# The largest-output pass of a quantized feed-forward layer: turned context split straight from PSUM by ScalarE and VectorE

## The chip, the cores and the metric

The program runs on one core of one Trainium2 chip. The metric is the device time of one execution in microseconds, the median over the runs shown.

## The reference, cut to what matters

The whole reference is two transformer layers. The pass that is changed is in the quantized feed-forward network of the first layer, and it also carries, beside it, the making of the second layer's keys.

```
# first layer's feed-forward network (act_qdq rounds to 16 bits with one scale for the whole tensor)
up   = act_qdq(x @ w_up.T)
gate = act_qdq(x @ w_gate.T)
gate = act_qdq(gate * fixed_qdq_u16(sigmoid(gate)))
o    = act_qdq(gate * up)          # its scale needs max |gate * up| over everything first
...
# second layer: q and k go through the same two projections
qp = (q @ W1.T + b1) @ W2.T + b2
kp = (k @ W1.T + b1) @ W2.T + b2   # k is ctx_1024, 16 x 256 rows of 512
```

The kernel folds both projections of q and k into one 512x512 matrix (`gram`) that is applied to the turned (transposed) context. The products are made in fp32r with operands split in a high part (the value rounded to fp32r) and a low part (value minus high part).

## The kernel before

`output_maximum` is the pass that finds the largest output. Its main loop runs over N = 48 pieces n of 128x1024 elements. Three engines work on a piece. SyncE (SP, the DMA queue) loads `raw(n)` (512 KB, two buffers) and, for odd n, the rounded sigmoids `sq(n)` (256 KB, one buffer). ScalarE (ACT) makes `up(n)` and, once VectorE has made the product, `gate(n)`; for odd n it also makes a sigmoid. VectorE (DVE) does, in its iteration n: for even n `rounded(n + 2)`; then `outputs(n)`, then `products(n + 2)`, then `largest(n)`. So `products(n)` is done in VectorE's iteration n - 2.

Beside it the second layer's keys are made. The context is 16 blocks x of 256 rows; a chunk c is two blocks. For each block SP loads `cin` (512 KB, one buffer), TensorE turns it into `ctp` in PSUM (`turn(x)`, 8 transposes), and it is split in a high and a low part in `cT` (memory of `qf_wd`, two buffers by c). In a chunk TensorE does turn(2c+2), key tile 0, key tile 1, turn(2c+3), key tiles 2 and 3, and the key biases `tb`; each tile is 12 matmuls of 128x512. ScalarE takes each key tile out of PSUM (`keys`) and SP stores it (256 KB).

What sets the order is the program order of each queue and the semaphores:

- In the version before, ScalarE copies `ctp` to `craw` in SBUF (L1587) and frees the PSUM by that (`c_out`); GpSimd (POOL) makes the high part by a cast (L1694) and the low part by a subtraction (L1696). `turn(x)` waits for `c_out`, x times.
- ScalarE does the copy for block x >= 2 in its piece n = 11 + 2x (`context_due`).
- SP works through its pieces in order. In piece n = 10 + 2x it issues raw(n), then `load_context(x)`, then a store of keys; in piece n = 11 + 2x it issues raw(n), then sq(n). `load_context(x)` waits until turn(x-1) is done, since there is one `cin`, and everything behind it in SP's queue waits with it:

```
if context_due(n + 1):
    load_context(context_due(n + 1))
...
def load_context(x):
    if x:
        sp.wait_ge(c_full, x)
```

Of the kernel before, what the change touches and what calls it, by code (L numbers as in the profile page):

```python
# [14 lines left out]
ALU = mybir.AluOpType  # L15
ACT = mybir.ActivationFunctionType
F32 = mybir.dt.float32
# [6 lines left out]
P = 128  # L24
B, S, D = 16, 256, 512
TOK = B * S
CT = 512
NCH = TOK // CT
NT = CT // P
KD = D // P  # L30
# [1396 lines left out]
def output_maximum(nc, a, ctx_in, keys_d, bias_d, raw_up, gate, sq_d, big, scal, folds, wd, wd_parts, wd_late, ident):  # L1427
# [9 lines left out]
    with Phase(nc, "om") as ph:  # L1437
# [13 lines left out]

        gram = ph.sb("gram", [P, 2, KD, D], F32R)
        cin = ph.sb("cin", [P, NK, D])
        craw = ph.sb("craw", [P, KD, S])
        rout = ph.sb("rout", [P, 2, CT])
        b12 = ph.sb("b12", [P, 2, KD])
        bsum = ph.sb("bsum", [P, KD])
# [16 lines left out]
            ph.sem(n) for n in ("turned", "turned_out", "m_full", "m_out", "beta_full", "beta_out", "g_full", "g_out", "gc_full", "gc_out"))  # L1474
        cleared, beta_ready, betas_ready, gram_hi, gram_low, gbraw_done, gb_hi, gb_low = (
            ph.sem(n) for n in ("cleared", "beta_ready", "betas_ready", "gram_hi", "gram_low", "gbraw_done", "gb_hi", "gb_low"))
        c_full, c_out, c_hi, c_low, r_full, r_out, t_full, t_out = (
            ph.sem(n) for n in ("c_full", "c_out", "c_hi", "c_low", "r_full", "r_out", "t_full", "t_out"))
        t_stored = [ph.sem(f"t_stored{i}") for i in range(2)]
        r_stored = [ph.sem(f"r_stored{i}") for i in range(2)]  # L1480

# [15 lines left out]
        with nc.Block() as block:  # L1497
# [69 lines left out]
            @block.scalar  # L1567
            def _(act):
                def sigmoid(n):
                    if n >= 2:  # L1570
                        act.wait_ge(sq_done, n // 2)
                    act.activation(sig[:], place(n), ACT.Sigmoid, scale=scal[:, S_G:S_G + 1]).then_inc(sig_ready, 1)

                def products(n):
                    s = n % 2
                    act.wait_ge(raw_ready[s], 16 * (n // 2) + 16)
                    if n >= 2:
                        act.wait_ge(out_done, n - 1)
                    act.activation(up[:, s, :], raw[:, s, :], ACT.Copy, scale=scal[:, I_U:I_U + 1]).then_inc(up_ready, 1)
                    act.wait_ge(prod_done, n + 1)  # L1580
                    act.activation(place(n), prod[:, s, :], ACT.Copy, scale=scal[:, I_A:I_A + 1]).then_inc(gate_ready, 1)

                def context(x):
                    act.wait_ge(c_full, x + 1)
                    if x:
                        act.wait_ge(c_low, x)
                    act.activation(craw[:], ctp[:], ACT.Copy).then_inc(c_out, 1)  # L1587

                def keys(c, i):
                    act.wait_ge(r_full, KD * c + i + 1)  # L1590
                    if c == 0 and i == 0:
                        act.wait_ge(gc_out, 2)
                        act.wait_ge(gb_low, 1)
                    if KD * c + i >= 2:
                        act.wait_ge(r_stored[i % 2], 16 * (2 * c + i // 2))
                    act.activation(rout[:, i % 2, :], rb[i][:], ACT.Identity, bias=gcol[:, i:i + 1]).then_inc(r_out, 1)

                def key_biases(c):
                    act.wait_ge(t_full, c + 1)
                    if c >= 2:  # L1600
                        act.wait_ge(t_stored[c % 2], 16 * (c // 2))
                    act.activation(trow[:, c % 2, :], tb[0:1, :], ACT.Identity, bias=bb[0:1, 0:1]).then_inc(t_out, 1)

                sigmoid(0)
                sigmoid(2)
                for n in range(N):
                    products(n)
                    if n % 2 and n + 3 < N:
                        sigmoid(n + 3)
                    if n == TURNED:  # L1610
                        for k in range(KD):
                            act.wait_ge(turned, k + 1)
                            act.activation(w2T[:, k, :], rb[k][:], ACT.Copy).then_inc(turned_out, 1)
                    if n == 3:
                        context(0)
                    if FOLDED <= n < FOLDED + KD:
                        act.wait_ge(m_full, n - FOLDED + 1)
                        act.activation(m[:, n - FOLDED, :], rb[n - FOLDED][:], ACT.Copy).then_inc(m_out, 1)
                    if n == 9:
                        act.wait_ge(beta_full, 1)  # L1620
                        act.activation(bsum[:], tb[:, 0:KD], ACT.Copy).then_inc(beta_out, 1)
                        context(1)
                    if 10 <= n < 10 + KD:
                        act.wait_ge(g_full, n - 9)
                        act.activation(graw[:, n - 10, :], rb[n - 10][:], ACT.Copy, scale=SCALE).then_inc(g_out, 1)
                    if n == 14:
                        act.wait_ge(gc_full, 1)
                        act.activation(gcol[:], tb[:, 8:8 + KD], ACT.Copy, scale=SCALE).then_inc(gc_out, 1)
                        act.activation(bb[:], tb[:, 16:17], ACT.Copy, scale=SCALE).then_inc(gc_out, 1)
                    if bias_due(n) is not None:  # L1630
                        key_biases(bias_due(n))
                    if keys_due(n):
                        keys(*keys_due(n))
                    if context_due(n):
                        context(context_due(n))
                key_biases(NCH - 1)

            @block.vector
            def _(dve):
# [6 lines left out]
                def products(n):  # L1646
                    s = n % 2
                    if s:
                        dve.wait_ge(sq_ready, 16 * (n // 2) + 16)
                    else:  # L1650
                        dve.wait_ge(sq_done, n // 2 + 1)
                    if n >= 2:
                        dve.wait_ge(gate_ready, n - 1)
                    dve.tensor_tensor(prod[:, s, :], place(n), sq[:, s, :], ALU.mult).then_inc(prod_done, 1)

                def outputs(n):
                    dve.wait_ge(gate_ready, n + 1)
                    dve.wait_ge(up_ready, n + 1)
                    if n:
                        dve.wait_ge(max_done, n)  # L1660
                    dve.tensor_tensor(outp[:], place(n), up[:, n % 2, :], ALU.mult).then_inc(out_done, 1)

                def largest(n):
                    dve.wait_ge(out_done, n + 1)
                    dve.tensor_reduce(mx[:, n:n + 1], outp[:], AX_X, ALU.max, apply_absolute_value=True).then_inc(max_done, 1)
# [4 lines left out]
                for n in range(N):  # L1670
                    if n % 2 == 0 and n + 2 < N:
                        rounded(n + 2)
                    outputs(n)
                    if n + 2 < N:
                        products(n + 2)
                    largest(n)
                dve.wait_ge(max_done, N)
                dve.tensor_reduce(mx_row[:], mx[:], AX_X, ALU.max).then_inc(row_max, 1)
# [5 lines left out]

            @block.gpsimd
            def _(pool):
                def context(x):
                    c, lo = x // 2, x % 2 * S
                    pool.wait_ge(c_out, x + 1)
                    if c >= 2:  # L1690
                        pool.wait_ge(t_full, c - 1)
                    if c == 1:
                        pool.wait_ge(gc_full, 1)
                    pool.tensor_copy(cT[c % 2][:, 0, :, lo:lo + S], craw[:]).then_inc(c_hi, 1)  # L1694
                    pool.wait_ge(c_hi, x + 1)
                    pool.tensor_tensor(cT[c % 2][:, 1, :, lo:lo + S], craw[:], cT[c % 2][:, 0, :, lo:lo + S].bitcast(F32), ALU.subtract).then_inc(c_low, 1)  # L1696

                pool.memset(betas, 1.0).then_inc(cleared, 1)
                pool.wait_ge(cleared, 1)
                pool.memset(gbraw, 1.0).then_inc(cleared, 1)  # L1700
                pool.wait_ge(cleared, 2)
                context(0)
                pool.wait_ge(b_ready, 32)
                pool.wait_ge(beta_out, 1)
                pool.tensor_tensor(beta[:], bsum[:], b12[:, 1, :], ALU.add).then_inc(beta_ready, 1)
                pool.wait_ge(beta_ready, 1)
                pool.tensor_tensor(betas, betas, beta[:].unsqueeze(2).broadcast_to([P, KD, P]), ALU.mult).then_inc(betas_ready, 1)
                context(1)
                for d in range(KD):
                    pool.wait_ge(g_out, d + 1)  # L1710
                    pool.tensor_copy(gram[:, 0, d, :], graw[:, d, :]).then_inc(gram_hi, 1)
# [6 lines left out]
                pool.tensor_copy(gb[:, 0], gbraw).then_inc(gb_hi, 1)  # L1718
                pool.wait_ge(gb_hi, 1)
                pool.tensor_tensor(gb[:, 1], gbraw, gb[:, 0].bitcast(F32), ALU.subtract).then_inc(gb_low, 1)  # L1720
                for x in range(2, 2 * NCH):
                    context(x)
                pool.wait_ge(row_max, 1)
                pool.partition_all_reduce(big[:, 0:1], mx_row[:], P, RMAX).then_inc(all_max, 1)

# [1 line left out]
            def _(pe):  # L1727
                def turn(x):
                    pe.wait_ge(c_ready, 16 * x + 16)
                    if x:  # L1730
                        pe.wait_ge(c_out, x)
                    for k in range(KD):
                        for t in range(NK):
                            ins = pe.transpose(ctp[:, k, t * P:(t + 1) * P], cin[:, t, k * P:(k + 1) * P], ident[:])
                    ins.then_inc(c_full, 1)
# [980 lines left out]
```

## Time and profile before

| what | value |
|---|---|
| median of 3 runs | 3637.34 us (3633.27 to 3641.07) |
| profiled execution, its own time | 3638.54 us |
| span of the profiled execution | 3636.9 us |
| PE busy | 3247.5 us, 89% |
| DVE busy | 1961.0 us, 54% |
| ACT busy | 1554.9 us, 43% |
| POOL busy | 828.2 us, 23% |

The pass that is changed lies between about 1960 and 2204 us of the span, 7% of it, so the shares above are those of other stages and say little of it. The median of the runs is 1.2 us under the profiled execution's time.

### The profile page before, as it was taken

Reading aid. Unit: us, or ns where it says so; the run is one execution under the profiler, and the core shown is the slowest. Engines: PE = TensorE matmul, PEld = TensorE weight load, DVE = VectorE, ACT = ScalarE, POOL = GpSimd, SP = SyncE. Lnnn points to the kernel's source line nnn. Section 1 sums busy time; section 2 is a strip of 40 time slices with the busy share of each in tenths; the row PEclk is TensorE's granted clock in tenths of the full one; section 3 lists DMA queues with packets and bytes.
Section 4 is the critical chain, followed back from the end, with each engine's and each line's share of the span. In section 5 each row is a group of like instructions: output and inputs, shape, how many; then the busy total and the mean of one; then the engine's idle time right before and its main releaser. Section 6 shows DMA issues by size and latency. Waiting matters only on the chain. (4 is left out here: it accounts for less than half of the span.)

```text
span 3636.9 us, 51541 instructions
## 1 busy us (share of the span) xinstructions
PE 3247.5 (89%) x17336; PEld 2773.5 (76%) x17336; DVE 1961.0 (54%) x3269; ACT 1554.9 (43%) x2939; POOL 828.2 (23%) x1134
## 2 busy tenths in 40 slices
PE   7999889999999987998996886995937999999998
PEld 6989788888888875886885665884825778777776
DVE  3245467777777754555888995554942222222221
ACT  3222266666666643334776775563631111111110
POOL 0000067666666640000000440002610000000000
PEclk9999989999999998998998898997977999999999
DMA  6577655444545426555666676443641000110000
GB/s 181 152 239 231 198 165 146 145 144 142 148 141 147 135 73 224 187 173 165 220 223 216 210 224 213 151 159 137 218 147 38 22 29 24 35 35 33 32 24 12
DMA packets 368405, 503.42 MB, mean 138 GB/s; under 512 B 58779, under 2 KB 233115, under 8 KB 363759
## 3 DMA queue, kind: packets, MB, share of 16 engines
q1 hardware_dynamic: 355418, 491.16, 42.9%
q0 software_dynamic: 2176, 8.39, 0.6%
q10 hardware_dynamic: 10592, 1.04, 0.3%
q8 instruction: 127, 2.08, 0.2%
q14 instruction: 92, 0.75, 0.1%
HBM read 292.83 MB, written 174.08 MB: 128 GB/s over the span
## 5 line engine op out<-in xcount | busy, mean ns | idle before, releaser
L2387 DVE SCALAR_TENSOR_TENSOR lf_hT<-lf_hb,lf_hT 128x512 fp32r<-128x512 f32 x128 | 88.5, 692 | 631.2 <-ACT lf_hT L2445 629.2
L2445 ACT ACTIVATE lf_hT<-lf_hb 128x512 fp32r<-128x512 f32 x128 | 76.6, 598 | 691.9 <-PE lf_py L185 641.9
L766 POOL TENSOR_TENSOR at_prob<-at_prob,at_rec 128x308 f32<-128x308 f32 (+1 forms) x256 | 261.5, 1044 | 265.7 <-DVE at_rec L808 265.3
L901 ACT ACTIVATE at_prob<-at_sc,at_nm 128x77 f32<-128x77 f32 (+1 forms) x1024 | 293.5, 383 | 41.7 <-DVE at_nm L795 41.7
L795 DVE TENSOR_REDUCE at_nm<-at_sc 128x4 f32<-128x308 f32 (+1 forms) x256 | 164.6, 685 | 172.3 <-PE at_sc L955 172.2
L914 ACT ACTIVATE at_pT<-at_tp 128x1024 fp32r<-128x1024 f32 x128 | 131.6, 1028 | 202.1 <-PE at_tp L965 202.1
L183 PE MATMUL lf_hb<-lf_xT,lf_w 128*128 128x512 f32 x512 | 204.5, 399 | 0.0
L184 PE MATMUL lf_hb<-lf_xT,lf_w 128*128 128x512 f32 x512 | 203.0, 396 | 0.0
L185 PE MATMUL lf_hb<-lf_xT,lf_w 128*128 128x512 f32 x512 | 202.9, 396 | 0.0
L184 PE MATMUL lf_py<-lf_w,lf_hT 128*128 128x512 f32 x512 | 202.5, 395 | 0.0
L185 PE MATMUL lf_py<-lf_w,lf_hT 128*128 128x512 f32 x512 | 202.4, 395 | 0.0
L183 PE MATMUL lf_py<-lf_w,lf_hT 128*128 128x512 f32 x512 | 202.3, 395 | 0.0
L183 PE MATMUL dn_py<-qf_wd,dn_om 128*128 128x512 f32 x384 | 150.4, 392 | 28.2 <-DVE dn_om L1865 28.2
L801 DVE TENSOR_REDUCE at_sums<-at_prob 128x4 f32<-128x308 f32 (+1 forms) x256 | 172.7, 675 | 0.0
L183 PE MATMUL pg_bank<-pg_xs,qg_wg 128*128 128x512 f32 x384 | 153.2, 399 | 20.0 <-DVE pg_xs L1359 20.0
L753 POOL TENSOR_TENSOR at_ks<-at_kr,at_ks 128x512 fp32r<-128x512 f32 x128 | 164.8, 1288 | 16.2 <-ACT at_ks L908 16.2
L812 DVE TENSOR_TENSOR at_pT<-at_tp,at_pT 128x1024 fp32r<-128x1024 f32 x128 | 156.1, 1220 | 22.8 <-ACT at_pT L914 22.8
L2327 POOL TENSOR_SCALAR lf_var<-lf_mv 128x1 f32<-128x1 f32 x32 | 7.1, 223 | 704.6 <-DVE lf_mv L2340 704.6
L183 PE MATMUL pu_bank<-pu_xs,qu_wu 128*128 128x512 f32 x384 | 151.0, 393 | 18.0 <-DVE pu_xs L1359 16.6
L183 PE MATMUL at_vq<-at_xT,xo_Wq 128*128 128x256 f32 x512 | 147.5, 288 | 18.2 <-DMA at_xT<-xn_parts 12.8
L183 PE MATMUL at_vq<-at_pT,at_vs 128*128 128x256 f32 x512 | 156.5, 306 | 0.9 <-DVE at_oT L818 0.8
L955 PE MATMUL at_sc<-at_ks,at_qs 128*128 128x256 f32 x1024 | 148.2, 288 | 5.0 <-DMA at_qs<-at_qst 4.9
(319 smaller groups left out, 9627.7 us busy)
## 6 DMA issues: line engine op xcount, KB each, us to landing
at_kr<-k_rows SPq DMA_DIRECT2D x256, 128.0 KB, 2.8
at_qs<-at_qst SPq DMA_DIRECT2D x512, 64.0 KB, 2.1
raw_gate<-pg_stage SPq DMA_DIRECT2D x96, 256.0 KB, 2.0
pu_rg<-raw_gate SPq DMA_DIRECT2D x96, 256.0 KB
raw_up<-pu_stage SPq DMA_DIRECT2D x96, 256.0 KB, 2.1
om_raw<-raw_up SPq DMA_DIRECT2D x48, 512.0 KB, 4.2
dn_raw<-raw_up SPq DMA_DIRECT2D x48, 512.0 KB, 3.8
xn_parts<-pr_xturned SPq DMA_DIRECT2D x32, 512.0 KB, 5.0
```

What stands on the lines that cost most here:

```text
L183: pe.matmul(out, lh, rh, start=start, stop=False, **kw)
L184: pe.matmul(out, lh, rl, start=False, stop=False, **kw)
L185: return pe.matmul(out, ll, rh, start=False, stop=stop, **kw)
L753: pool.tensor_tensor(ks[:, n % NK, :, 1, :], kr[:, n % NKR], ks[:, n % NK, :, 0, :].bitcast(F32), ALU.subtract).then_inc(k_low, 1)
L766: ins = pool.tensor_tensor(prob[:, i, :, lo:hi], prob[:, i, :, lo:hi], rec[:, z, g, :].unsqueeze(2).broadcast_to([P, 2 * NTE, hi - lo]), A ...
L795: ins = dve.tensor_reduce(nm[:, n % 2, g, :], sc[n % 2][:, :, lo:hi], AX_X, ALU.max, negate=True)
L801: dve.tensor_reduce(sums[:, z, g, :], prob[:, i, :, SEG[g][0]:SEG[g][1]], AX_X, ALU.add).then_inc(sum_done, 1)
L812: dve.tensor_tensor(pT[:, n % 2, 1], tp[:], pT[:, n % 2, 0].bitcast(F32), ALU.subtract).then_inc(pt_done, 1)
L901: ins = act.activation(prob[:, i, m, lo:hi], sc[n % 2][:, m, lo:hi], ACT.Exp, bias=nm[:, n % 2, g, m:m + 1])
L914: act.activation(pT[:, n % 2, 0], tp[:], ACT.Copy).then_inc(pt_hi, 1)
L955: ins = pe.matmul(sc[n % 2][:, h * NTE + m, :], qs[:, n % NQ, h, m * P:(m + 1) * P], ks[:, n % NK, h, part, :], start=part == 0, stop=part ...
L2387: dve.scalar_tensor_tensor(hT[:, i, 1, :], hb[i][:], 0.0, hT[:, i, 0, :].bitcast(F32), ALU.max, ALU.subtract).then_inc(h_done, 1)
```

## The change

ScalarE's activation writes the high part directly into `cT`, VectorE makes the low part from PSUM and the high part, and GpSimd has no part in the split. `craw` and `c_out` are gone. `turn(x)` now waits for `c_low` (the low part of the block before) and no longer for ScalarE's copy alone. VectorE's subtraction for block x >= 2 stands in its iteration n = 12 + 2x, after `products(n + 2)` and before `largest(n)`; those of blocks 0 and 1 stand in iterations 4 and 10.

```diff
@@ scalar
                 def context(x):
+                    c, lo = x // 2, x % 2 * S
                     act.wait_ge(c_full, x + 1)
-                    if x:
-                        act.wait_ge(c_low, x)
-                    act.activation(craw[:], ctp[:], ACT.Copy).then_inc(c_out, 1)
+                    if c >= 2:
+                        act.wait_ge(t_full, c - 1)
+                    if c == 1:
+                        act.wait_ge(gc_full, 1)
+                    act.activation(cT[c % 2][:, 0, :, lo:lo + S], ctp[:], ACT.Copy).then_inc(c_hi, 1)
@@ vector
+                def context_low(x):
+                    c, lo = x // 2, x % 2 * S
+                    dve.wait_ge(c_hi, x + 1)
+                    dve.tensor_tensor(cT[c % 2][:, 1, :, lo:lo + S], ctp[:], cT[c % 2][:, 0, :, lo:lo + S].bitcast(F32), ALU.subtract).then_inc(c_low, 1)
...
                     if n + 2 < N:
                         products(n + 2)
+                    if n == 4:
+                        context_low(0)
+                    if n == 10:
+                        context_low(1)
+                    if context_due(n - 1):
+                        context_low(context_due(n - 1))
                     largest(n)
@@ gpsimd
-                def context(x):
...
-                    pool.tensor_copy(cT[c % 2][:, 0, :, lo:lo + S], craw[:]).then_inc(c_hi, 1)
-                    pool.wait_ge(c_hi, x + 1)
-                    pool.tensor_tensor(cT[c % 2][:, 1, :, lo:lo + S], craw[:], cT[c % 2][:, 0, :, lo:lo + S].bitcast(F32), ALU.subtract).then_inc(c_low, 1)
...
-                for x in range(2, 2 * NCH):
-                    context(x)
@@ tensor
                 def turn(x):
                     pe.wait_ge(c_ready, 16 * x + 16)
                     if x:
-                        pe.wait_ge(c_out, x)
+                        pe.wait_ge(c_low, x)
```

On VectorE, iterations 18 and 19 (the place of block 3; each later pair of iterations up to 43 has the same order) stood before as follows. `om_sq` is rounded(20), `om_outp` outputs, `om_prod` products, `om_mx` largest.

```order
L1644 TENSOR_SCALAR om_sq<-om_sig 128x1024
L1661 TENSOR_TENSOR om_outp<-qf_gate,om_up 128x1024
L1654 TENSOR_TENSOR om_prod<-qf_gate,om_sq 128x1024
L1665 TENSOR_REDUCE om_mx<-om_outp 128x1
L1661 TENSOR_TENSOR om_outp<-qf_gate,om_up 128x1024
L1654 TENSOR_TENSOR om_prod<-qf_gate,om_sq 128x1024
L1665 TENSOR_REDUCE om_mx<-om_outp 128x1
```

In the changed program the same place reads:

```order
L1646 TENSOR_SCALAR om_sq<-om_sig 128x1024
L1668 TENSOR_TENSOR om_outp<-qf_gate,om_up 128x1024
L1656 TENSOR_TENSOR om_prod<-qf_gate,om_sq 128x1024
L1661 TENSOR_TENSOR qf_wd<-om_ctp,qf_wd 128x4x256
L1672 TENSOR_REDUCE om_mx<-om_outp 128x1
L1668 TENSOR_TENSOR om_outp<-qf_gate,om_up 128x1024
L1656 TENSOR_TENSOR om_prod<-qf_gate,om_sq 128x1024
L1672 TENSOR_REDUCE om_mx<-om_outp 128x1
```

One subtraction (`qf_wd<-om_ctp,qf_wd`) has come in between the even iteration's product and its largest; the next product, `products(21)`, which reads sq(21), is the fourth row behind it.

SP's queue keeps its order. At the place of pieces 20 and 21 it reads, before and now alike (line numbers of the changed program):

```order
L1505 DMA om_raw<-raw_up 128x1024
L1514 DMA om_cin<-in_ctx_dram 128x2x512
L1518 DMA folded_keys<-om_rout 128x2x256
L1505 DMA om_raw<-raw_up 128x1024
L1509 DMA om_sq<-gate_sigmoids 128x1024
L1518 DMA folded_keys<-om_rout 128x2x256
```

Nothing moved here: behind the load of the context block 5 (`om_cin`), which waits for turn(4), stand a store of keys, raw(21) and sq(21).

## Rows read from the trace of the kernel before

**Rows 1.** Windows, pieces 16 to 40: length; busy PE, PEld, DVE, ACT, POOL; clock; DMA share, GB/s

```profile
2048.00:2170.00 122.00, 103.99 (x455) 83.11 (x454) 118.62 (x86) 94.54 (x104) 51.37 (x24) 0.92 0.76 243
```

**Rows 2.** Groups by line, 2048 to 2170 us: busy us, mean ns | idle before

```profile
L1654 DVE TENSOR_TENSOR om_prod<-qf_gate,om_sq 128x1024 f32<-128x1024 int16 x25 | 55.6, 2225 | 1.8 <-DMA om_sq<-gate_sigmoids 1.8
L1696 POOL TENSOR_TENSOR qf_wd<-om_craw,qf_wd 128x1024 fp32r<-128x1024 f32 x12 | 37.9, 3158 | 1.0
```

**Rows 3.** Timeline of VectorE and GpSimd, iterations 18 and 19: start us, us

```profile
2057.91 1.21 DVE L1654 TENSOR_TENSOR om_prod<-qf_gate,om_sq 128x1024 f32<-128x1024 int16 x1
2059.05 1.20 DVE L1665 TENSOR_REDUCE om_mx<-om_outp 128x1 f32<-128x1024 f32 x1
2060.39 1.32 DVE L1661 TENSOR_TENSOR om_outp<-qf_gate,om_up 128x1024 f32<-128x1024 int16 x1
2060.71 3.25 POOL L1696 TENSOR_TENSOR qf_wd<-om_craw,qf_wd 128x1024 fp32r<-128x1024 f32 x1
2061.63 3.41 DVE L1654 TENSOR_TENSOR om_prod<-qf_gate,om_sq 128x1024 f32<-128x1024 int16 x1
2064.97 1.21 DVE L1665 TENSOR_REDUCE om_mx<-om_outp 128x1 f32<-128x1024 f32 x1
2066.09 0.68 DVE L1644 TENSOR_SCALAR om_sq<-om_sig 128x1024 uint16<-128x1024 f32 x1
2066.69 1.21 DVE L1661 TENSOR_TENSOR om_outp<-qf_gate,om_up 128x1024 f32<-128x1024 int16 x1
2067.83 1.21 DVE L1654 TENSOR_TENSOR om_prod<-qf_gate,om_sq 128x1024 f32<-128x1024 int16 x1
```

**Rows 4.** Timeline of VectorE: products(18) and products(42), 12 pairs apart

```profile
2048.04 1.21 DVE L1654 TENSOR_TENSOR om_prod<-qf_gate,om_sq 128x1024 f32<-128x1024 int16 x1
...
2169.49 1.21 DVE L1654 TENSOR_TENSOR om_prod<-qf_gate,om_sq 128x1024 f32<-128x1024 int16 x1
```

**Rows 5.** Timeline of TensorE and SP: turn(4), sq(21), turn(5), load of block 6, sq(23)

```profile
2049.80 1.06 PE L1734 MATMUL om_ctp<-ident,om_cin 128*128 128x128 f32 x8
...
2055.15 0.34 SPq L1510 DMA_DIRECT2D om_sq<-gate_sigmoids  x1
...
2062.44 1.03 PE L1734 MATMUL om_ctp<-ident,om_cin 128*128 128x128 f32 x8
...
2063.51 0.38 SPq L1515 DMA_DIRECT2D om_cin<-in_ctx_dram  x1
...
2065.07 0.37 SPq L1510 DMA_DIRECT2D om_sq<-gate_sigmoids  x1
```

**Rows 6.** DMA, issue to landing: sq(23), sq(27), and all 24 sq loads

```profile
om_sq<-gate_sigmoids SPq DMA_DIRECT2D x1, 256.0 KB, 5.1
...
om_sq<-gate_sigmoids SPq DMA_DIRECT2D x1, 256.0 KB, 6.6
...
DMA to landing us min/median/max: 2.9/4.3/10.2
```

**Rows 7.** Timeline of TensorE after idle times: turn(2), then key tile 0 of chunk 1

```profile
2031.96 1.97 PE L1734 MATMUL om_ctp<-ident,om_cin 128*128 128x128 f32 x8 [9.80 <-POOL om_gram L1713]
...
2054.10 0.79 PE L183 MATMUL om_rb<-qf_wd,om_gram 128*128 128x512 f32 x1 [3.23 <-POOL qf_wd L1696]
...
2059.81 0.47 PE L184 MATMUL om_rb<-qf_wd,om_gram 128*128 128x512 f32 x1
```

**Rows 8.** One line's instructions (another stage): duration ns min/median/max

```profile
L812 DVE TENSOR_TENSOR at_pT<-at_tp,at_pT x128: 1212/1224/1226, 484.3 to 1341.7; 128x1024 fp32r<-128x1024 f32 x128
```

**Rows 9.** Timeline of VectorE under GpSimd's first and third subtraction

```profile
1995.46 3.38 DVE L1654 TENSOR_TENSOR om_prod<-qf_gate,om_sq 128x1024 f32<-128x1024 int16 x1
...
2040.89 3.22 DVE L1661 TENSOR_TENSOR om_outp<-qf_gate,om_up 128x1024 f32<-128x1024 int16 x1
```

**Rows 10.** Timeline at the pass's end: last key biases, loads of down weights, next stage's start

```profile
2194.61 0.66 ACT L1602 ACTIVATE qf_fold<-om_tb,om_bb 1x512 f32<-1x512 f32 x1
...
2197.24 0.83 SPq L1529 DMA_DIRECT2D qf_wd<-wd_parts  x2
...
2213.35 1.15 ACT L1841 ACTIVATE dn_up<-dn_raw,scal 128x1024 int16<-128x1024 f32 x1 [18.08 <-DMA dn_raw<-raw_up]
```

More of the change, by code:

```diff
@@ L1453, in output_maximum @@
         cin = ph.sb("cin", [P, NK, D])
-        craw = ph.sb("craw", [P, KD, S])
         rout = ph.sb("rout", [P, 2, CT])
@@ L1476, in output_maximum @@
             ph.sem(n) for n in ("cleared", "beta_ready", "betas_ready", "gram_hi", "gram_low", "gbraw_done", "gb_hi", "gb_low"))
-        c_full, c_out, c_hi, c_low, r_full, r_out, t_full, t_out = (
-            ph.sem(n) for n in ("c_full", "c_out", "c_hi", "c_low", "r_full", "r_out", "t_full", "t_out"))
+        c_full, c_hi, c_low, r_full, r_out, t_full, t_out = (
+            ph.sem(n) for n in ("c_full", "c_hi", "c_low", "r_full", "r_out", "t_full", "t_out"))
         t_stored = [ph.sem(f"t_stored{i}") for i in range(2)]
@@ L1686, in _ @@
             def _(pool):
-                def context(x):
[L1688 to L1693, printed above, removed]
-                    pool.tensor_copy(cT[c % 2][:, 0, :, lo:lo + S], craw[:]).then_inc(c_hi, 1)
-                    pool.wait_ge(c_hi, x + 1)
-                    pool.tensor_tensor(cT[c % 2][:, 1, :, lo:lo + S], craw[:], cT[c % 2][:, 0, :, lo:lo + S].bitcast(F32), ALU.subtract).then_inc(c_low, 1)
                 pool.memset(betas, 1.0).then_inc(cleared, 1)
@@ L1701, in _ @@
                 pool.wait_ge(cleared, 2)
-                context(0)
                 pool.wait_ge(b_ready, 32)
@@ L1707, in _ @@
                 pool.tensor_tensor(betas, betas, beta[:].unsqueeze(2).broadcast_to([P, KD, P]), ALU.mult).then_inc(betas_ready, 1)
-                context(1)
                 for d in range(KD):
```

## The prediction

> **What bounds the pass now.** The busy shares of the whole span show TensorE, but they are those of other stages; so I read the windows of this pass first. Between 2048 and 2170 us VectorE is busy 118.6 of 122 us, TensorE 104, ScalarE 94.5, GpSimd 51, the DMA engines 76% [rows 1]. VectorE sets the pace. The groups by line say what it spends: the 25 products take 2225 ns each [rows 2], where an undisturbed one takes 1.21 us [rows 3, 4]. The timeline shows why: products(21) starts at 2061.63, ends only at 2065.04, and GpSimd's subtraction runs from 2060.71 to 2063.96 [rows 3]; the product ends 1.08 us after it, one product's length. Each of GpSimd's subtractions (3158 ns, 12 of them in this stretch [rows 2]) holds up one product by about 2.2 us. From products(18) to products(42), 12 pairs of iterations, it is 121.45 us [rows 4], 10.12 us a pair.
>
> By the Trainium skill ("SBUF — State Buffer", section "Who interferes with whom"), a VectorE instruction with two SBUF inputs and a GpSimd one that reads SBUF exclude each other for a whole instruction, and one with a single SBUF input stays clear. The trace agrees (3.41 against 1.21 us).
>
> The second thing to read is what SP's queue does around turn(x-1). Block 5's load waits for turn(4). Before, turn(4) begins at 2049.80, in VectorE's iteration 17, while SP is far ahead: sq(21) is issued at 2055.15, the moment products(19) has freed its buffer, and is not needed before 2061.63 [rows 3, 5]. SP's queue has slack because turn(x-1) waits for nothing of VectorE's.
>
> **What the change removes and adds, VectorE alone.** The intervals between starts in a pair are 1.14 (product to largest), 1.34, 1.14 (clean; 1.24 in the row), 1.14 for a clean product (3.34 in the row), 1.12, 0.60, 1.14 [rows 3]. Clean, that is 7.6 us. The new subtraction from PSUM does not stand in this pass; the nearest row is the same form elsewhere, 1224 ns [rows 8], and it would take about 1.2 us of the pair at the interval of like instructions. So VectorE's own work falls from 10.12 to 8.8 us a pair. ScalarE's activation keeps its size and only writes elsewhere: nothing. GpSimd's work vanishes; nobody else waits for it there.
>
> **What the change moves: a wait.** turn(x-1) now waits for context_low(x-2), in VectorE's iteration 8+2x. SP's load of block x waits for turn(x-1). Behind it in SP's queue stand a key store, raw(11+2x) and sq(11+2x), and sq(11+2x) is what VectorE's iteration 9+2x needs for its product. That closes a ring: VectorE, TensorE, SP, DMA, VectorE, inside four VectorE instructions. I walk one pair from the start of products(10+2x), time 0:
>
> - context_low starts at 1.14 and ends at 2.36 [rows 3, 8].
> - turn(x-1) starts about 0.05 later. TensorE has then been idle for 2 to 5 us (below), and after idle times it is slow: a turn after 9.8 us idle took 1.97 us against 1.03 to 1.06, and after 3.23 us idle 13 matmuls took 5.71 us, 0.44 each, while the next 11 took 2.63, 0.24 each [rows 5, 7]. I take 1.97: done at 4.4.
> - The context load is issued at once (2063.51 behind a turn that ended at 2063.47), sq 1.56 us later (2065.07), with the key store and raw between them [rows 5]: at 6.0.
> - Landing: 5.1 us in just this burst of 1.5 MB; another burst took 6.6, the median of all is 4.3 [rows 6]. I take 5.1, since the queue has run empty by then: sq lands at 11.1.
> - VectorE, which could have begun the product at 1.14 + 1.14 + 1.34 + 1.14 = 4.8, has stood still for 6.3 us. Then 1.14 + 1.12 + 0.60 + 1.14 = 4.0 to the next even product: a pair takes **15.1 us**.
>
> ScalarE is inside this: its context(x-1) follows the turn at 4.4, then up, gate and a key tile, about 4 us, before raw(11+2x) lands at 10.5; its next gate is ready long before VectorE's next even output needs it. TensorE per chunk: two key tiles after one turn, 24 matmuls, and 36 after the other; at 0.24 with the first 13 at 0.44 that is 8.4 and 11.2 us behind turns that end at 4.4, so it is done at 12.8 and 15.6, when the next low part comes at 15.1 + 2.4 = 17.5. It is idle 2 to 5 us before each turn, which is why I called it slow; for the shorter of these that is a choice.
>
> The ring exists for the loads of blocks 4 to 15, so 12 pairs, exactly those from products(18) to products(42): 12 x 15.1 = 181 against 121.45, **+59.7 us**. In one of them (piece 24) 1 MB of down weights stands before raw and sq; at 243 GB/s [rows 1] that is 4.3 us more, less what it already costs now: **+3**.
>
> **Head and tail.** Before products(18) the three GpSimd subtractions held VectorE up by 2.2, 2.9 and 2.0 us (the first and third stand in [rows 9]; the second lies between them and hit two instructions); two of VectorE's own come in, 2.3 us: **-4.8**. After products(42) (2169.49) the last key biases were taken at 2194.61, 25.1 later, the last weight loads issued at 2197.24 and the next stage begun 16.1 us behind them, at 2213.35 [rows 4, 10]. Now turn(15) ends at 4.4, 36 matmuls take it to 15.6, chunk 7's 60 matmuls at 0.24 to 30.0, and the biases come then instead of at 25.1: **+4.9**, which the weight loads hand on to the next stage.
>
> Sum: 59.7 + 3 - 4.8 + 4.9 = +62.8. On the profiled execution's 3638.5 that is 3701.3; the median lies 1.2 lower, so **3700 us**.
>
> **The rivals.**
>
> *Only the relief counts (faster).* If SP were still far ahead, VectorE would gain 12 x 1.3 = 15.4 and the head's 4.8: 3617 us, or 3622 with the later tail. For it: VectorE is the bound and the hold-up is plain in [rows 2, 3]. Against it: sq would have to land by 4.8, and the turn ahead of its issue is over only at 3.5 to 4.4; no sq load landed in under 2.9 us [rows 6]. It decides only if sq is issued before the context load, and the queue's order says it is not. 5%. The exclusion rule of the skill, named above, speaks for this rival and is silent on the ring.
>
> *The ring with TensorE at full speed.* The turn takes 1.06: 0.9 us less in each of 12 pairs, 3689. Idle times of 2 to 5 us lie around the 3.23 that were enough to slow it [rows 7]; 15%.
>
> *The ring with a slow TensorE that becomes late.* If its 36 matmuls all go at 0.44, they are done at 4.4 + 15.8 = 20.2, 2.7 past the low part, in six chunks: +16, 3716. 12%.
>
> *The burst lands as the worse one.* 6.6 in place of 5.1: 12 x 1.5 = +18, 3718. 12%. With the median landing, 4.3, it is -10, 3690; 8%.
>
> *The ring partly hidden, so that it only eats the gain (3637).* It takes a stall of 1.3 us a pair, which no landing time above gives; 3%.
>
> **How the numbers follow.** My forecast as it stands has 45%. Low end: full-speed turns and median landings, 3679, and the tail's 4.9 gone: 3674. High end: late TensorE and some slow landings: 3722. A change of 0.2% (7.3 us) is about what a measurement of this kernel can tell from none. Faster 0.05, same 0.02, slower 0.93.
>
> **What would show it.** Right: VectorE's odd products wait for the DMA of `om_sq`, 12 times, about 6 us each, some 75 us together (1.8 before [rows 2]); products(18) to products(42) about 181 us; products of 1.21 us; the context load issued right behind a turn and the turn right behind a low part; lower granted clock in this pass. Wrong: no such wait and a pair of 8.8 us; or a ring closed elsewhere, say VectorE waiting for ScalarE's gate.

## The result and the profile after

The changed kernel takes 3702.52 us (median of 4 runs, 3698.07 to 3707.1) against 3638.87 us for the kernel before on the same chip (four runs, one more than in the table above): ratio 1.0177, 95% interval 1.0159 to 1.0195, slower by some 64 us. Its profiled execution took 3698.07 us with a span of 3696.4 us, 59.5 us more than before. The forecast was 3700 us, between 3674 and 3722.

The window from products(18) to products(42) answers to [rows 1, 4]. It was 121.45 us and is now 185.17, 15.43 us a pair. The columns are those of [rows 1].

```profile
2041.71:2226.88 185.17, 122.25 (x456) 98.43 (x456) 104.51 (x97) 89.88 (x102) 0.00 (x0) 0.78 0.47 157
```

No engine is full any more: VectorE is busy 104.5 of 185 us, GpSimd does nothing, the granted clock fell from 0.92 to 0.78, the DMA engines' share from 0.76 to 0.47. This is what a ring of waits looks like. Who waits for whom in this window (us in total, times, longest; the last row is the DMA queue's own wait):

```profile
ACT om_rout L1598 <- DMA folded_keys<-om_rout: 91.5, 13, 8.6
DVE om_prod L1656 <- DMA om_sq<-gate_sigmoids: 79.1, 12, 8.4
PEld om_ctp L1732 <- issue: 69.4, 12, 9.4
PE om_ctp L1732 <- DVE qf_wd L1661: 64.6, 12, 9.0
...
SPq L1514 <- PE om_ctp L1732: 97.4, 12, 12.2
```

TensorE's turn waits for VectorE's low part, SP's load of the context waits for the turn, and VectorE's product waits for the DMA of `om_sq`, 12 times each: three edges of the ring. The groups by line show that the products themselves are what they should be (1222 ns in place of the 2225 of [rows 2]); what was in the product is now in front of it:

```profile
L1656 DVE TENSOR_TENSOR om_prod<-qf_gate,om_sq 128x1024 f32<-128x1024 int16 x24 | 29.3, 1222 | 79.1 <-DMA om_sq<-gate_sigmoids 79.1
```

One round of the ring in the timeline (from products(28) to products(30), with turn(8) and the load of block 9; rows of the ring only):

```profile
2119.05 1.22 DVE L1656 TENSOR_TENSOR om_prod<-qf_gate,om_sq 128x1024 f32<-128x1024 int16 x1
2120.18 1.22 DVE L1661 TENSOR_TENSOR qf_wd<-om_ctp,qf_wd 128x1024 fp32r<-128x1024 f32 x1
...
2121.55 1.94 PE L1732 MATMUL om_ctp<-ident,om_cin 128*128 128x128 f32 x8 [3.92 <-DVE qf_wd L1661]
...
2123.52 0.38 SPq L1514 DMA_DIRECT2D om_cin<-in_ctx_dram  x1
2123.95 0.47 SPq L1518 DMA_DIRECT2D folded_keys<-om_rout  x1
2124.46 0.47 SPq L1505 DMA_DIRECT2D om_raw<-raw_up  x1
2124.97 0.46 SPq L1509 DMA_DIRECT2D om_sq<-gate_sigmoids  x1
...
2130.61 1.23 DVE L1656 TENSOR_TENSOR om_prod<-qf_gate,om_sq 128x1024 f32<-128x1024 int16 x1 [6.72 <-DMA om_sq<-gate_sigmoids]
...
2134.62 1.22 DVE L1656 TENSOR_TENSOR om_prod<-qf_gate,om_sq 128x1024 f32<-128x1024 int16 x1
```

Read downward: the low part ends at 2121.40 and the turn begins 0.15 later; SP's four DMAs go out the moment the turn ends (2123.49); sq lands 5.6 us after its issue and the product begins that instant. The next even product is 15.57 us behind the first.

### The profile page after: what moved, and what is told of

Its sections match the earlier page's. It is cut to its first block and busy times, and to the rows that moved or that the text cites. A ratio compares the mean times of both kernels' runs of the same rounds, so it can differ in the third digit from the quotient of the medians.

```text
span 3696.4 us, 51508 instructions
## 1 busy us (share of the span) xinstructions
PE 3262.9 (88%) x17336; PEld 2786.9 (75%) x17336; DVE 1943.4 (53%) x3285; ACT 1551.5 (42%) x2939; POOL 760.1 (21%) x1102
## 3 DMA queue, kind: packets, MB, share of 16 engines
q10 hardware_dynamic: 10592, 1.04, 0.3%
```

## The experiments

Each was measured beside the kernel before, on the same chip; the medians of the kernel before were 3641.12 us (e1 to e4), 3639.71 (e5 to e8) and 3637.78 (e9, e10). Since the chips differ, two kernels of different groups are best compared by their ratios: 0.001 is 3.6 us. The table gathers them; "pair" is the distance from products(18) to products(42) in each profile, divided by 12.

| kernel | median us | ratio to before (95%) | pair us |
|---|---|---|---|
| before | 3637.78 to 3641.12 | 1 | 10.12 |
| changed | 3702.52 | 1.0177 (1.0159 to 1.0195) | 15.43 |
| e1 changed, context load behind sq | 3637.41 | 0.9995 (0.9985 to 1.0004) | 10.10 |
| e2 before, context load behind sq | 3640.54 | 0.9995 (0.9985 to 1.0005) | 9.90 |
| e3 changed, low part one iteration earlier | 3652.98 | 1.0033 (1.0020 to 1.0045) | 11.45 |
| e4 changed, sq ahead of raw in odd pieces | 3686.49 | 1.0121 (1.0104 to 1.0138) | 14.08 |
| e5 changed, e1 and e3 together | 3622.55 | 0.9951 (0.9934 to 0.9967) | 9.19 |
| e6 e5, sq ahead of raw and of its wait | 3617.86 | 0.9933 (0.9916 to 0.9950) | 8.94 |
| e7 before, GpSimd casts in place of subtracting | 3622.75 | 0.9956 (0.9939 to 0.9973) | 9.51 |
| e8 changed, TensorE kept busy | 3698.80 | 1.0161 (1.0144 to 1.0178) | 15.04 |
| e9 before, SP's order of e6 | 3632.44 | 0.9985 (0.9975 to 0.9996) | 9.89 |
| e10 changed, SP's order of e6 | 3629.96 | 0.9975 (0.9964 to 0.9986) | 9.48 |

### e1_load_later and e2_before_load_later: open the ring at SP

```diff
-                    if context_due(n + 1):
-                        load_context(context_due(n + 1))
+                    if context_due(n):
+                        load_context(context_due(n))
```

> The changed kernel, with SP's load of context block x moved from piece 10+2x to piece 11+2x, behind raw(11+2x) and sq(11+2x); nothing else. My theory (the ring VectorE low part, turn, SP's load of the context, sq behind it, VectorE's product): sq no longer stands behind the turn, the ring is open, and VectorE's own work is left, 8.8 us a pair in place of 15.4 (185.2 us from products(18) to products(42)). 106 us there, 79 less: about 3623 us, below the kernel before. Rival (TensorE's slow clock, or VectorE's added instruction itself, makes the pair long): TensorE and VectorE do the same work in the same order, so the pair stays near 15 us: 3690 us or more.

> Control: the same move of the context load in the kernel before the change. My theory: there the turn waits for ScalarE's copy alone, sq is never late, so the move has nothing to free: 3639 us, within 4. Rival (the order of loads is simply bad, whatever the split): it gains 10 us or more here too, 3629 or less.

e1 took 3637.41 us. One line of SP's order takes back all 64 us, with VectorE's, ScalarE's and TensorE's programs untouched, so the rival (added work or the clock as the cause) falls. But it is 14 us short of what was expected: a pair is 10.1 us and not 8.8. e2 is as forecast, 3640.54: where the turn does not wait for VectorE, no gain shows in the time. In its one profile the 12 pairs are 2.6 us shorter (118.80 in place of 121.45), which its median does not show.

The waits of e1 between the same two products say what was left:

```profile
PE om_ctp L1732 <- DVE qf_wd L1661: 22.8, 9, 8.1
ACT om_rout L1598 <- DMA folded_keys<-om_rout: 20.9, 12, 2.5
DVE om_prod L1656 <- DMA om_sq<-gate_sigmoids: 15.1, 11, 2.7
ACT qf_wd L1589 <- PE om_ctp L1732: 10.5, 8, 3.8
```

sq is still late, by 1.4 us on average, and ScalarE now waits for the turn. That gave a second theory, a longer ring through ScalarE: low part, turn, ScalarE's copy, up(n-2), raw(n), sq(n). e5, e6 and e10 test it.

### e3_low_earlier: shorten the ring at VectorE

```diff
-                    if context_due(n - 1):
-                        context_low(context_due(n - 1))
+                    if context_due(n):
+                        context_low(context_due(n))
```

> The changed kernel, with VectorE's low part of block x in iteration 11+2x in place of 12+2x, right behind products(13+2x); SP's order stays. My theory gives the pair by the ring's length: from the low part's start to the landing of sq it is 9.9 us in the trace (2105.12 to 2115.04), then one product, 1.1, and the next low part follows at once: 11.1 us a pair, 133 us in place of 185: about 3651 us. Rival (it is the landing alone, a burst that must be waited out, wherever the low part stands): no change, 3702. Rival (the ring is hidden by this one step): 8.8 us a pair, 3623.

3652.98 us, 11.45 us a pair (137.4 us between the two products). The ring's length was 11.1 by rows of the changed kernel's trace; the pair that also carries the load of 1 MB of down weights took 15.64 by itself, and the other 11 took 11.07 on average. The number separates the three readings: the wait is neither a fixed burst nor hidden by one step.

### e4_sq_first: shorten the ring in the DMA queue

```diff
-                    sp.dma_start(raw[:, n % 2, :], ...)
                     if n % 2:
                         if n >= 2:
                             sp.wait_ge(prod_done, n - 1)
                         sp.dma_start(sq[:, 1, :], ...)
+                    sp.dma_start(raw[:, n % 2, :], ...)
```

> The changed kernel, with sq(n) issued before raw(n) in odd pieces; all waits stay. My theory: the ring loses raw's issue (0.5 us) and its 512 KB ahead of sq in the queue (1.7 us at some 300 GB/s): 2.2 us a pair, 12 pairs, 26 us: about 3676 us, each of VectorE's waits near 4.2 us in place of 6.4. If ScalarE, which now gets raw later, ends the wait instead, less is won: 3690. Rival (the wait is for the turn and not for what is queued): no change, 3702.

3686.49 us: the right way, but 16 us less than the changed kernel (16.2 in the window, 20 by the two ratios) and not 26. In the round shown, the ring from the low part to the product is 1.6 us shorter and not 2.2; over the 12 pairs it is 1.35:

```profile
2108.57 1.22 DVE L1661 TENSOR_TENSOR qf_wd<-om_ctp,qf_wd 128x1024 fp32r<-128x1024 f32 x1
...
2112.89 0.41 SPq L1508 DMA_DIRECT2D om_sq<-gate_sigmoids  x1
2113.35 0.50 SPq L1509 DMA_DIRECT2D om_raw<-raw_up  x1
...
2117.41 1.22 DVE L1656 TENSOR_TENSOR om_prod<-qf_gate,om_sq 128x1024 f32<-128x1024 int16 x1 [5.14 <-DMA om_sq<-gate_sigmoids]
```

sq lands 4.5 us after its issue here and 5.6 in the pair of the changed kernel shown above. My step that 512 KB less ahead of it save their 1.7 us of transfer was wrong: it saves about 1.1. The 1.7 came from an estimated rate; between 2125 and 2130 us, in the burst shown above, the changed kernel's DMA engines moved 330 GB/s.

### e5, e6, e9, e10: the second ring, and which edit opens it

e5 has the edits of e1 and e3. e6 adds this in SP's piece; e10 is e6 without e3's edit; e9 is the kernel before with e1's edit and this one.

```diff
+                    if n % 2:
+                        if n >= 2:
+                            sp.wait_ge(prod_done, n - 1)
+                        sp.dma_start(sq[:, 1, :], ...)
                     if n >= 2:
                         sp.wait_ge(up_ready, n - 1)
                     sp.dma_start(raw[:, n % 2, :], ...)
-                    if n % 2:
...
```

> The changed kernel with both moves: SP's context load in piece 11+2x behind sq (as in e1_load_later, 3637 us, 10.1 us a pair) and VectorE's low part in iteration 11+2x (as in e3_low_earlier, 3653 us, 11.3). e1's trace left short waits for sq, up to 2.7 us, because sq(n) stands behind raw(n), which waits for ScalarE's up(n-2), and ScalarE stands waiting for the turn and for its key stores. My theory: a second ring through ScalarE (low part, turn, ScalarE's copy, up, raw, sq) of about 10 us; with the low part one iteration earlier the turn comes 3.6 us earlier and this ring is shorter than VectorE's own 8.8: about 3622 us. Rival (those waits are the DMA engines' own, at over 240 GB/s, whoever issues when): no better than e1, 3637.

> e5's kernel, and SP issues sq(n) before it waits for up(n-2) and issues raw(n). My theory: sq is then late behind nothing of ScalarE's; if e5 still has waits for sq, they go: 8.8 us a pair, 3620 us, a few us or nothing under e5. Rival (DMA engines are the limit): as e5.

> The kernel before the change with SP's new order of e6_sq_before_raw (context load behind sq, sq ahead of raw); GpSimd keeps the split. Theory: VectorE is the bound there by GpSimd's hold-ups, 10.1 us a pair, and SP's order frees nothing: 3640 us, within 4. Rival (e6's gain of 22 us over the kernel before is SP's order and not the split): near 3618.

> The changed kernel with SP's new order of e6, and VectorE's low part where the change put it (iteration 12+2x). It stands between e1_load_later (3637) and e6 (3618) and tells which of the two edits removed e1's second ring. If that ring went through ScalarE's late up(n-2) and raw to sq, sq ahead of raw opens it: 3622. If the late turn itself costs (ScalarE and the key tiles wait for it), it stays near 3635.

e5: 3622.55 us, as forecast, 9.19 us a pair. e6: 3617.86 us, 8.94 a pair, faster than the kernel before by 0.7% and than the changed one by some 2.4% (by the ratios). VectorE is full again (103.7 of 107.3 us), and the DMA engines move 265 GB/s, more than before, so their own limit was not what held e1:

```profile
2050.67:2157.97 107.30, 97.01 (x449) 78.34 (x448) 103.70 (x97) 88.87 (x99) 0.00 (x0) 0.96 0.87 265
```

e10, 3629.96 us and 9.48 a pair, lies in the middle: with sq ahead of raw the waits for sq all but go (2.7 us in total, in the window of the 12 pairs), but TensorE still waits 18.8 us for the low part and VectorE 5.7 us for ScalarE's gate. SP's context load still waits 25.5 us for turns there, against 29.0 in e1, so it was not this wait that made sq late in e1 but raw's wait for ScalarE (56.1 us in e1). The low part one iteration earlier took away the rest (e6). So both branches of the second ring were real: raw's wait for ScalarE, and the late turn itself; that the late turn is what makes ScalarE's gate late in e10 is argued from the order and was not tested alone.

e9, 3632.44 us, is faster than the kernel before by 0.15% (interval 0.04 to 0.25%), with a pair of 9.89, and just outside what was expected of it (3640, within 4). Of e6's 22 us some 5 are SP's order alone. The split off GpSimd by itself does not bring the rest: e10 and e9 have the same SP order, differ in the split, and their intervals overlap. It pays once the low part stands one iteration earlier too.

### e7_cast_only: the price of GpSimd's subtraction

```diff
-                    pool.tensor_tensor(cT[c % 2][:, 1, :, lo:lo + S], craw[:], cT[...][:, 0, ...].bitcast(F32), ALU.subtract).then_inc(c_low, 1)
+                    pool.tensor_copy(cT[c % 2][:, 1, :, lo:lo + S], craw[:]).then_inc(c_low, 1)
```

> The kernel before, with GpSimd's subtraction replaced by a second cast of craw into the low part (the low part of the context is wrong by that, so the second layer's keys are too); all waits and the number of instructions stay. It measures what GpSimd's subtraction costs VectorE. My theory (a two-input subtraction holds a two-input product up, 2.2 us each for 12, 7 more in the head): up to 33 us less, 3608, if a cast holds nothing up; 3620 if the second cast costs a product about 1 us. Rival (the long products are not GpSimd's doing): 3641.

This kernel does not make the low part; its place holds the high part a second time. It takes 3622.75 us, 17 less than before and near the 3620 expected if a second cast costs about 1 us. The groups by line from 2048 to 2165 us:

```profile
L1654 DVE TENSOR_TENSOR om_prod<-qf_gate,om_sq 128x1024 f32<-128x1024 int16 x25 | 36.4, 1455 | 16.4 <-DMA om_sq<-gate_sigmoids 16.4
...
L1696 POOL CAST qf_wd<-om_craw 128x1024 fp32r<-128x1024 f32 x12 | 21.3, 1778 | 0.8
```

The product falls from 2225 ns [rows 2] to 1455, 25 x 0.77 = 19 us; the rest of its excess over 1.22 us lies in 9 products of 1.35 to 2.02 us, each of which overlaps a cast. The second cast is held up as well: 10 of the 12 took 1.9 to 2.0 us, against 1.04 of an undisturbed one. But 16.4 us of waits for sq appear, against 1.8: with VectorE faster, something else begins to bind. From products(18) to products(42) SP's raw loads, which stand ahead of sq, waited 74.5 us for ScalarE's `up` and its context loads 4.1 us for turns; which of the two makes sq late was not tested here. By the Trainium skill ("SBUF — State Buffer", section "Who interferes with whom") a VectorE instruction with two SBUF inputs contends with any GpSimd one that reads SBUF, a cast as well; the two rows agree.

### e8_tensor_kept_busy: the clock's part of the ring

```diff
                         if i % 2 == 0 and c + 1 < NCH:
+                            if c or i:
+                                fill = 20 if i else 12
+                                for q in range(fill):
+                                    pe.matmul(idle[:], gram[:, 0, 0, 0:P], gram[:, 0, 0, :], start=q == 0, stop=q == fill - 1)
                             turn(2 * c + 2 + i // 2)
```

> The changed kernel with 12 or 20 matmuls more (128x512, into a PSUM bank that nobody reads) ahead of each turn from block 3 on, in the time in which TensorE stood idle for 3 to 4 and 6 to 8 us. My theory: the ring contains the turn, 1.94 us after such idle times; TensorE kept busy turns in 1.03 to 1.06, so 0.9 us less in each of 12 pairs: 11 us under the changed kernel, 3692. Rival (the turn's speed is not in the ring): 3703. If the added work reaches past the low part, it costs: 3705 or more.

3698.80 us, 15.04 us a pair against 15.43: 4.7 us less in the 12 pairs in place of 11. The added matmuls run at once and leave 1 to 4.6 us of idle time before the turns. Only 8 of the 12 turns were quick (1.06 to 1.07 us); the other four took 1.86 to 1.94 and stood behind 2.7 to 4.6 us of idle time. The transposes took 324 ns on average against 416 in the changed kernel, where all but one turn took 1.87 to 1.94 us.

```profile
L1733 PE MATMUL om_ctp<-ident,om_cin 128*128 128x128 f32 x96 | 16.2, 324 | 31.4 <-DVE qf_wd L1662 31.4
```

VectorE's waits for sq fell with it, from 79.1 to 74.4 us. The granted clock in the window was 0.95, against 0.78 in the changed kernel, and a pair still took 15.04 us: the low clock is not the cause of the ring. The turn's speed is a link of it, by estimate worth 0.9 us a pair (1.94 less 1.06). The 4.7 us are from one profile of each kernel; the intervals of the two ratios (e8 and changed) overlap. How long the ring is with every turn quick was not reached.

## Why the prediction was right

**The bound before** held: GpSimd's subtraction in the product was real (e7), VectorE the pace-setter. VectorE's own work in a clean pair, put at 8.8 us, is 8.75 in the clean pairs of e5 and e6.

**The ring** was the step on which all rested, and e1 shows it by opening it, e3 and e4 by shortening it at two other places. The mechanism is in the trace edge by edge. Two places were counted one too far: products(21) is the third row behind the subtraction in the listing above, not the fourth, and turn(4) began in VectorE's iteration 16 before, not 17; nothing in the sum hangs on either. Size, part by part (the first four rows from the round shown above):

| term | predicted | measured |
|---|---|---|
| low part starts, after the product's start | 1.14 | 1.13 |
| turn ends | 4.4 | 4.44 |
| sq issued | 6.0 | 5.92 |
| sq lands, product starts | 11.1 | 11.56 |
| a pair | 15.1 | 15.57 there, 15.43 on average |
| products(18) to products(42) | +62.7 with the 1 MB load | +63.7 |
| head | -4.8 | -5.0 |
| tail | +4.9 | +1.3 |

The 62.7 are two terms. The 11 pairs without the 1 MB load took 15.27 us in place of 15.1, which is 2.0 more over 12; the pair with it took 17.24, so the load cost 2.0 in place of 3.

The turn took 1.94 us against the 1.97 taken. The choice to call all turns slow was right for a reason a little different from mine: TensorE was idle for 3.2 to 4.2 us before half of them, where my own sums give 1.9 (15.6 to 17.5), and 6 to 9 before the others, where I had 4.7.

The head is the distance from products(0) to products(18), 86.12 us before (1961.92 to 2048.04) and 81.11 now. **The tail** is the term that was off. The key biases did come later, 28.3 us behind products(42) in place of 25.1, and so did the weight loads, 30.9 in place of 27.8, which is +3.2. But the next stage began 14.25 us behind the loads and not 16.1, so only 1.3 of it were passed on. That a later issue is paid in full was wrong. The next stage's first instruction waited for the DMA of `dn_raw`, not for the weights: that load was issued 7.2 us behind the last weight loads before and 6.1 now, and landed 8.9 us later before and 8.15 now. Why both were shorter was not tested.

```profile
2255.17 0.66 ACT L1604 ACTIVATE qf_fold<-om_tb,om_bb 1x512 f32<-1x512 f32 x1
...
2257.82 1.30 SPq L1528 DMA_DIRECT2D qf_wd<-wd_parts  x3
...
2272.07 1.15 ACT L1839 ACTIVATE dn_up<-dn_raw,scal 128x1024 int16<-128x1024 f32 x1 [16.23 <-DMA dn_raw<-raw_up]
```

The sum of the parts is 63.7 - 5.0 + 1.3 = 60.0, against 59.5 between the two spans. The forecast was 62.8: the tail, 3.6 too high, was in part made up by the window, 1.0 too low. The medians differ by 63.6, within the spread of single runs (3633 to 3641, 3698 to 3707); that they lie nearer to the forecast than the two spans do is luck.

**The rivals.** "Only the relief counts" gave 3617 us; that is near e6's time, and what stands between is the order of SP's queue and the place of the low part. Short of both moves other waits bind (e1, e7, e10). The rival of a late TensorE did not come: all 12 turns waited for VectorE. One branch was sized wrong: I had ScalarE copy the block right behind the turn, at 4.4. The key stores stand behind the context load as well, and ScalarE waited 91.5 us for their landing. In the round shown it began the copy at 2129.35, 10.3 us behind the product. It ended 5.4 us before VectorE's next low part, so nothing was lost. In the changed kernel ScalarE's gates are in time too (VectorE never waits for them); in e10 VectorE does, 5.7 us.

## What to carry to other kernels

- When a buffer's release moves from one engine to another, follow it to the queue that reloads the buffer, and list everything that stands behind that load. Here turn(4) began 1.8 us behind products(18) before and 17.3 us behind it in the changed kernel. That alone is not what cost the 64 us, for in e1 the turn still waits for the low part; behind the load stood the very operand that the new releaser needs three instructions later.
- A ring of waits can be costed link by link from rows of the old trace. The sign here that one had closed was that no engine was full and that VectorE, TensorE and SP each waited 12 times, once for each of the 12 context loads in the ring.
- A fix that opens one ring is worth measuring for the next one: e1 gave 65 us and then stood at 10.1 us a pair; e5 and e6 found another 15 and 20.

## What was not expected of the hardware

- What is issued just ahead of a transfer moved its landing by less than the 1.7 us that I had estimated for those bytes. With 512 KB less ahead of it sq landed after 4.5 in place of 5.6 us in the two rounds shown; the medians over all 24 sq loads are 4.0 us with raw issued behind sq (e4) and 5.1 with raw ahead of it (changed kernel).
- A GpSimd cast with one input holds up a two-input VectorE product as the subtraction does, only for less time: the longest product in e7's 12 pairs took 2.06 us, against 3.4 under a subtraction and 1.22 clean (1455 ns on average).
